# Node run of a fused graph network: the degree column sent two pieces per node group, six edge groups gathered in two parts

## The reference, cut to what matters

```python
h = maximum(layernorm(x), 0)                      # (100000, 64)
# layer 0, on h:
x = layernorm(h) * ln_gamma + ln_beta
deg = segment_sum(edge_weight, src)               # per node
dinv = where(deg > 0, 1 / sqrt(deg), 0)           # the degree factor, per node
w = -(dinv[src] * edge_weight * dinv[dst])        # per edge
prop(h) = segment_sum(w[:, None] * h[src], dst)   # used twice
```

## Time and profile before

| What | us |
|---|---|
| median of 3 runs | 5643.91 (5642.55 to 5646.13) |
| span of the profiled execution, first to last instruction | 5641.0 |
| node run in it: ACT's first piece, POOL's first gather | 549.8, 550.5 |
| node run in it: last x1 store issued | 1175.85 |
| node run in it: last gather issued, last `d_xd` store issued | 1192.7, 1196.2 |
| next phase in it: first load issued | 1204.42 |

### The profile page before, as it was taken

How to read it: one execution, slowest core, us unless ns; L and a number is a source line. 1 busy time by engine, 2 the same in 40 slices (tenths; PEclk the granted TensorE clock), 3 DMA queues, 4 the chain that set the end, 5 groups by cost and what they waited for, 6 DMA issues and landing times. The chain is left out here.

```text
span 5641.0 us, 69641 instructions
## 1 busy us (share of the span) xinstructions
PE 3732.6 (66%) x15267; PEld 1851.4 (33%) x15267; DVE 4168.8 (74%) x6266; ACT 2361.1 (42%) x4957; POOL 3788.1 (67%) x3734
## 2 busy tenths in 40 slices
PE   8997788847776999677727876777555546552110
PEld 3443555533332333244414442333222212221000
DVE  8876789957774555788868988999655559996442
ACT  0000678833331222466618973343222247772221
POOL 7776766767775777577724337666377767774777
PEclk9998899977876555788869998899766568885555
DMA  5533987744442222455524433333244423332221
GB/s 59 77 53 56 153 203 226 234 136 107 107 106 55 61 63 61 141 182 171 181 64 129 137 117 76 82 83 82 79 130 131 131 69 76 76 73 65 68 72 51
DMA packets 538641, 595.34 MB, mean 106 GB/s; under 512 B 300576, under 2 KB 315046, under 8 KB 536923
## 3 DMA queue, kind: packets, MB, share of 16 engines
q1 hardware_dynamic: 319004, 473.91, 28.7%
q0 software_dynamic: 115712, 91.82, 9.1%
q10 hardware_dynamic: 103840, 28.71, 4.2%
HBM read 354.69 MB, written 303.31 MB: 117 GB/s over the span
## 5 line engine op out<-in xcount | busy, mean ns | idle before, releaser
L1135 POOL DMA_INDIRECT l_got<-d_x,l_near x1176 | 1157.6, 984 | 557.5 <-issue 354.6
L1135 POOL DMA_INDIRECT p_got<-d_h,p_near x392 | 440.2, 1123 | 155.8 <-issue 118.9
L848 PE MATMUL ps<-hot_lo,hot_w 128*128 128x512 bf16 x2352 | 510.0, 380 | 13.4 <-DVE hot_lo L785 13.4
L1135 POOL DMA_INDIRECT p_got<-d_sums,p_near x392 | 401.4, 1024 | 151.7 <-issue 149.3
L2457 POOL DMA_INDIRECT out<-fi_res,fi_near x392 | 381.0, 972 | 181.1 <-issue 118.2
L726 POOL DMA_INDIRECT d_pos<-place,near x392 | 400.2, 1021 | 125.2 <-issue 119.1
L1135 POOL DMA_INDIRECT p_got<-d_ext,p_near x392 | 382.2, 975 | 132.4 <-issue 117.1
L1143 POOL DMA_INDIRECT ln_xd<-d_xt,idsE x304 | 286.9, 944 | 136.8 <-issue 96.9
L2131 PE MATMUL ps<-l_hid,w2n 128*64 128x512 f32 x392 | 234.8, 756 | 162.2 <-DVE l_sums L1308 155.7
L412 PE MATMUL ps<-ident,fi_sums 64*128 64x64 f32 x392 | 53.1, 314 | 424.8 <-DVE fi_sums L1308 424.8
L848 PEld LDWEIGHTS ps<-hot_lo,hot_w 128*128 128x128 bf16 x2352 | 230.6, 98 | 293.2 <-issue 17.3
(11 more groups left out here) (391 smaller groups left out, 10871.3 us busy)
## 6 DMA issues: line engine op xcount, KB each, us to landing
l_xd<-d_x SPq DMA_DIRECT2D x147, 256.0 KB
d_ext<-ln_ext SPq DMA_DIRECT2D x98, 264.0 KB
d_xt<-in_x_wide ACTq DMA_DIRECT2D x49, 520.0 KB
ln_x<-in_x SPq DMA_DIRECT2D x98, 256.0 KB
d_h<-ln_hb SPq DMA_DIRECT2D x98, 256.0 KB, 2.9
d_x<-ln_x SPq DMA_DIRECT2D x98, 256.0 KB
lb_x<-d_x SPq DMA_DIRECT2D x49, 512.0 KB
d_x<-lb_x SPq DMA_DIRECT2D x49, 512.0 KB
```

The lines of the kernel that those rows point to most:

```text
L848: last = nc.tensor.matmul(bank(h), hot_w[:, r, k], hot_lo[:, r, 512 * h:512 * h + 512], start=False, stop=False)
L1135: nc.gpsimd.indirect_dma_start(out=out[:, q], out_offset=None, in_=source, in_offset=bass.IndirectOffsetOnAxis(ap=ids[:, q:q + 1], axis=0) ...
```

## The change

The pieces go out two per node group, in the first 16 steps in place of the first 32, and the edge groups that are gathered as x and factor apart are six in place of eleven. `xd_turn` and `landed_by` use `TWICE` and follow it: edge groups 40 and 48 now have turns 94 and 108.

```diff
-TWICE = 11
+TWICE = 6
+COLUMN_TURNS = COLUMN_PARTS // 2
...
                 def columns(i, r, g):
-                    if isinstance(g, int) and g < COLUMN_PARTS:
-                        act.dma_start(column[g], factors[:, g].unsqueeze(2), allow_slow_non_contiguous=True
-                                      ).then_inc(m["columns"], 16)
+                    if isinstance(g, int) and g < COLUMN_TURNS:
+                        for k in (2 * g, 2 * g + 1):
+                            act.dma_start(column[k], factors[:, k].unsqueeze(2), allow_slow_non_contiguous=True
+                                          ).then_inc(m["columns"], 16)
...
-                ring_loop(act, NODE_GROUPS, [begin, columns], [scale], [base, tables], [mean], lead=COLUMN_PARTS, ring=NODE_RING)
+                ring_loop(act, NODE_GROUPS, [begin, columns], [scale], [base, tables], [mean], lead=COLUMN_TURNS, ring=NODE_RING)
```

## The result

The changed kernel takes 5662.28 us (median of five runs, 5658.94 to 5668.86), the kernel before 5643.91 on the same chip: the medians are 18.4 us apart, and the ratio on record over all runs is 1.0038, 95% interval 1.0026 to 1.0050. The changed kernel is slower. The forecast was +5.7 us, with no change within 0.2% (0.48) the likeliest case and slower by more than that (0.38) the next. It is the second that came; the time lies inside the range, in its upper half, 4 us under what the upper bound of T alone gives.

A forecast was written before the change was run, and what follows sets the result against it. Bound by the chain through DVE, ACT and PE without pieces, held up by transfers with them. Node run +24.3 us, tail -18.6: net +5.7 on 5643.9 gives 5649.6, rounded 5650; range 5628 to 5677.

The forecast's parts named there:

- T: Length of a node-run step with two pieces: taken as 10.0 us, bounds 8.8 to 11.2, alone giving 5633 to 5666.
- The mechanism: On ACT's queue a pair's second issue waits for the first piece; that hold is on the node run's path.
- second rival: Both issues of a step are held: T = 12 to 14.1 us, 5677 to 5707 us; given 22%.
- the first (a cheap second issue): Rival: ACT's queue takes two pieces, second issue costs 0.3 to 0.5 us, step 8.5, total 5629; given 13%.
- Until the first piece has nearly drained: How long ACT's second issue waits: 3.5 us for a lone piece, 4.3 and 5.9 behind a burst.
- D: The second issue's wait in a step, added to ACT's 5.3 us: 3.5 to 5.9 us, taken as 4.7.
- the sign of being right: Of the 32 piece issues on ACT, about half take 0.33 us and half 2.5 to 5.
- second way: Step from DMA work: 4.2 us plus two pieces of 3.0 makes 10.2, at share 1.03 9.9 us per step.
- The startup: Steps 0 and 1 of the node run cost nothing, since ACT idles there for x anyway, 8.19 us.
- 1200.2: Forecast time of the node run's last store: 1175.85 plus 24.3 us.
- POOL and the tail: POOL idles 40 us, hidden by the node run; three stores of 0.45 us follow the last x1 store.
- 24.3 - 18.6 = 5.7: Node run 24.3 us longer, less 18.6 us of removed edge-group store tail at the phase's end.

The follow-up runs named there:

- The nine groups with two queues: Version with nine groups in two parts and closer turns, every second piece issued from SP's queue: 1.0017, 5646.01 us.
- no column: Kernel before without the column's pieces and POOL's wait for them, the factor column left out of the computation: 0.9948, 5610.19 us.
- halves, two per step: Kernel before with each piece cut into two halves, both issued back to back in the same step, 32 steps as before: 1.0012.
- one piece, from two queues by turns: Kernel before with every second piece issued from SP's queue in place of ACT's: 1.0019.
- pair, from two queues: Changed kernel with the second piece of each pair issued from SP's queue: 1.0022 against the kernel before.
- pair in every second step: Kernel before with its 32 pieces over 32 steps, two back to back in each even step: 1.0080, 5683.98 against 5639.66 us.
- pair, second in mid-step: Changed kernel with the second piece issued in the middle of ACT's step, not back to back: 1.0039 against the kernel before.
- pair per step, eleven groups: Changed kernel with eleven edge groups in two parts again, so only the pairs are left: 1.0101, 5703.12 against 5647.98 us for the kernel before.
- piece and small load: Kernel before plus a load of 256 bytes behind each piece on ACT's queue: 1.0057, 5694.71 against 5664.73 us.
- nine groups and earlier turns: Kernel before with nine edge groups in two parts and earlier, closer store turns, one piece per step: 0.9969, 5621.60 against 5639.66 us.

## Why the prediction was right and where it was short

Node runs of the kernels in which the column's way out was changed, by their traces (holds: ACT's waits on "issue" up to the column's end; all in us). The nine groups with two queues are left out, since there SP waits for POOL ahead of the last store.

| kernel | node run | over no column | holds on ACT |
|---|---|---|---|
| no column | 589.4 | | |
| before: one piece per step | 626.0 | 36.7 | 23.4 |
| halves, two per step | 623.8 | 34.4 | 29.5 |
| one piece, from two queues by turns | 624.6 | 35.2 | none; SP held instead |
| pair, from two queues | 652.4 | 63.0 | 10.7; SP held too |
| pair in every second step | 660.6 | 71.2 | 45.4 |
| pair, second in mid-step | 663.3 | 73.9 | 74.2 |
| changed: pair per step | 667.6 | 78.2 | 81.6 |
| pair per step, eleven groups | 674.0 | 84.5 | 85.0 |
| piece and small load | 679.6 | 90.2 | 76.5 |

The traces come from several chips, so differences of a few us between rows mean nothing, and the last row holds the unexplained 24 us told above.

*The mechanism* of the forecast is shown as far as it carried the sum: the second issue is held, and that hold is on the path. The small load shows it without any work for the engines, the pair in every second step without any more work, and the two queues show that it goes with the queue. Of 16 pairs the first issue is free from pair 4 on, so the second rival (both held) came in pairs 1 and 2 alone, and the first (a cheap second issue) not at all.

What the hold waits for is another matter. "Until the first piece has nearly drained" describes the pairs: from pair 4 on 2567 to 3046 of the first piece's 3136 packets have moved when the hold ends, in the pair shown 2964 (ACT's queue from 625.18 to 631.16):

```profile
q10 hardware_dynamic: 2964, 0.01, 31.5%
```

It does not describe the small load, let in at about half, nor the half piece, let in with next to nothing moved, and not every pair in every second step (1934 to 3058 packets). On average the hold is 2.1 us behind a half piece, 3.6 for a small load and 4.1 for a second piece behind a whole one, and 5.4 in the changed kernel, pair upon pair. So it grows with the transfer ahead, though not with that alone; what the issuing engine waits for in that time stays open.

The sentence quoted from the Trainium skill, "DMA: Bandwidth & Descriptors", section "Issuing engines are not separate DMA queues", that issuing is "usually small relative to the DMA itself", does not hold here: 4.30 to 6.67 us of an issuing engine per pair, and 3.60 us for a load of 256 bytes. The same page's section "Queues, rings and completion order" says that SP and ACT each own one queue row; the two-queue run agrees, with 0.33 us for ACT's issues and 6.11 us for SP's.

*The drain was mis-sized*: D in T = 5.3 + D. I took 4.7, nearer to the shorter of two pieces behind a burst. From a pair's first issue to L1124 it is 6.08 us in the pair shown and 6.0 on average over the 12 steps from pair 3 to pair 15, a little over my upper bound of 5.9; 7 of the 12 holds from pair 4 on are longer than the 5 us that I gave as the sign of being right. The other term is 4.9 instead of 5.3, which hides a part of it. T is 10.9 instead of 10.0, and 12 steps of 0.9 make 11 us. My reason was that a hold can end a little before the last packet; by the counts above it does, with a tenth of the packets left, and D is long all the same. What I left out is the step ahead: against the second rival I had held that the second piece runs ahead of SP's next burst, and it doesn't. The pair in every second step measures D where the step ahead carries no piece: 4.5 us on average over the 13 pairs from 594 on, close to my 4.7. So the excess comes with pairs in step upon step. Stretches of 1 us in the changed kernel behind the hold that ends at 631.2, then in the kernel with the small loads behind the hold that ends at 631.5 (the last three columns are PEclk, DMA share, GB/s):

```profile
634.00:635.00 1.00, 1.00 (x3) 0.34 (x2) 0.00 (x0) 0.19 (x1) 0.77 (x1) 0.50 0.86 29
635.00:636.00 1.00, 1.00 (x6) 1.00 (x5) 0.47 (x1) 1.00 (x3) 0.69 (x2) 0.50 1.38 161
636.00:637.00 1.00, 1.00 (x7) 1.00 (x6) 0.52 (x3) 1.00 (x3) 0.69 (x2) 0.50 1.38 172
...
639.00:640.00 1.00, 1.00 (x8) 0.71 (x7) 1.00 (x3) 0.00 (x0) 0.78 (x1) 1.00 1.12 208
```

```profile
636.00:637.00 1.00, 1.00 (x10) 1.00 (x10) 0.61 (x1) 1.00 (x4) 0.92 (x1) 0.97 0.88 290
637.00:638.00 1.00, 1.00 (x8) 0.66 (x6) 0.92 (x3) 1.00 (x3) 0.77 (x1) 1.00 1.06 380
638.00:639.00 1.00, 1.00 (x9) 0.76 (x8) 1.00 (x2) 0.05 (x1) 0.70 (x2) 1.00 1.06 381
```

With pairs the second piece is still moving at 635 to 637 when SP's burst comes: the share is 1.38 at 161 and 172 GB/s, and the burst is at 208 GB/s as late as 639. The next pair, issued at 636.55, waits behind it: from there to 639 ACT's queue moves 75 packets. With nothing but a small load in the second place the burst goes at 380 GB/s and has its bulk through by 639. So the second piece delays SP's burst, and the burst the next pair. That this is the whole of the 1.3 us in D is argued from these rows; the pair in every second step shows only that D is short when no pair went ahead. The "second way" that confirmed T = 10.0 was wrong too: it priced a piece at a share of busy time. In the changed kernel from 600 to 700, 58493 small packets took 56.0% of 16 engines, 15.3 ns each; in the kernel before 44416 took 30.4%, 11.0 ns each. So the share of a queue is not a fixed cost per piece here.

```profile
q10 hardware_dynamic: 58493, 0.23, 56.0%
```

```profile
q10 hardware_dynamic: 44416, 0.18, 30.4%
```

(The queue that carries the pieces, packets, MB and share, in the changed kernel and in the kernel before, 600 to 700 us.)

*The startup was costed at nothing* and is not. ACT idles there for x, but both issues of pair 1 are held, the first for 7.81 us with SP's first loads issued just ahead of it, and pair 2 goes out at 567.61 instead of 564.45. There both are held again, and that step takes 13.0 us instead of 10.0. Pair 3 should have come at 574.45 and came at 580.61, 6.2 us late. With the 10.9 us of the steps that is the whole of the 17.1 us by which the last `d_x<-ln_x` store missed 1200.2; from pair 15 to the end, 505.8 us, both agree within 1 us.

*POOL and the tail* went as forecast. POOL stood idle 55 us, not 40, because the column was later; its last gather came at 1187 and not before 1160, because it waited 37.2 us for its buffers' stores, whose turns had moved with the node run; both are hidden by the node run, whose last store comes 30 us after that gather. The tail is three stores in 1.42 us. Taking six groups is neutral by itself (1.0006), and with pairs it gives back some 37 us by the times of the pairs alone and of both.

*The sum*: 41.5 us of node run, less a tail that went from 20.3 us (1175.85 to 1196.2) to 1.4 (1217.34 to 1218.7), is 22.5 us by the last store issued, where the forecast had 24.3 - 18.6 = 5.7. The next phase's first load moved by 19.6 us (1204.42 to 1224.03) and the median by 18.4. The removed part was sized right within half a microsecond; the added one was short by 17 us: 11 of them are the longer steps, 6 the startup.

## What to carry over

A saving at a phase's end must be set against what it costs the work ahead of it: the tail of 20 us could be had by nine groups and earlier turns of the stores, without the pairs (-18 us), and was bought here with 41 us of node run. Price a back-to-back issue by what stands in the issuing engine's queue and by what that engine holds up, and look at whether the second transfer will still be running when the next burst comes; one slow transfer per step, spread over as many steps as there are, cost half of what the same transfers cost in pairs. When a price per transfer is derived from a busy share, test it on a stretch with another mix before it is allowed to confirm a sum.

## What the runs showed that I had not expected

A load of 256 bytes behind a piece of 98 x 32 values of 4 bytes is held 3.60 us in the median, nearly as long as a second piece in every second step (4.1 us), and half a piece behind half a piece 2 us, on ACT's queue; behind a piece on SP's queue it is 3.15 to 7.33 us. The hold ends with anything from none to nearly all of the first transfer's packets moved, so it is not simply the drain. And ACT can be held 2 us in every step of 7.0 with hardly any loss (halves, 1.0012), while 3.6 us in every step cost 30 us in 32 steps, 0.9 us each (the small load). That short holds fall into time in which the node run waits for the transfers in any case would explain it; no run here tests that.
